# Weighted graph pass: one TensorE signal for each group of eight tiles, and GpSimd up to three groups ahead of the sums

## The reference, cut to what matters

```python
messages = edge_val[:, None] * embeddings[edge_src]
neighbor_emb = jax.ops.segment_sum(messages, edge_dst, num_segments=embeddings.shape[0])
```

## Time and profile before

| what | value |
|---|---|
| median of 3 runs | 9111.19 us (9107.15 to 9111.99) |
| profiled execution, its own time | 9109.78 us |
| its span, first to last instruction | 9108.0 us |
| mean granted TensorE clock | 0.752 of full |
| weighted pass, first gather to last addition | 4296.5 us to about 6910 us |
| gathers of the weighted pass | 1664, 950 ns each |
| scatters that stand between them | 164 |

### The profile page before, as it was taken

How to read it: one execution, slowest core, us unless ns; L and a number is a source line. 1 busy time by engine, 2 the same in 40 slices (tenths; PEclk the granted TensorE clock), 3 DMA queues, 4 the chain that set the end, 5 groups by cost and what they waited for, 6 DMA issues and landing times. The chain is left out here.

```text
span 9108.0 us, 108743 instructions
## 1 busy us (share of the span) xinstructions
PE 5754.6 (63%) x27644; PEld 4851.7 (53%) x27645; DVE 3952.2 (43%) x10086; ACT 1583.3 (17%) x3574; POOL 5514.8 (61%) x5737
## 2 busy tenths in 40 slices
PE   3677777777782588881444334444442489998994
PEld 3566656666662477771333333333332478888883
DVE  4566566777776400004444334444432432222225
ACT  1122121221120233330000000000000133333331
POOL 3566666666665466665666666666666246666662
PEclk7777777777775699995776776666766768888786
DMA  3333333333333144443332222222221022222335
GB/s 112 85 88 87 87 86 86 86 86 87 87 86 109 50 146 145 146 148 112 91 93 82 82 82 82 82 83 82 82 82 29 22 60 67 67 67 64 67 67 163
DMA packets 428356, 799.62 MB, mean 88 GB/s; under 512 B 129927, under 2 KB 267899, under 8 KB 427982
## 3 DMA queue, kind: packets, MB, share of 16 engines
q0 software_dynamic: 237808, 481.17, 21.3%
q1 hardware_dynamic: 190430, 317.21, 10.4%
HBM read 726.97 MB, written 70.98 MB: 88 GB/s over the span
## 5 line engine op out<-in xcount | busy, mean ns | idle before, releaser
L739 POOL DMA_INDIRECT g_G<-table,X x1664 | 1620.5, 974 | 944.0 <-issue 447.1
L1036 PE MATMUL g_pM<-g_G,g_S 128*128 128x256 f32 x3328 | 1111.0, 506 | 1674.8 <-DVE g_S L837 1371.4
L748 POOL DMA_INDIRECT g_G<-table,g_IDX x1664 | 1580.8, 950 | 843.2 <-issue 483.4
L1036 PEld LDWEIGHTS g_pM<-g_G,g_S 128*128 128x128 f32 x3328 | 854.2, 263 | 1931.6 <-DVE acc L857 1443.1
L1006 PE MATMUL g_pM<-g_G,g_S 128*128 128x260 f32 x3328 | 1205.7, 503 | 589.6 <-DVE acc L849 558.2
L1579 POOL DMA_INDIRECT q_G<-table,slot x1072 | 1038.1, 968 | 596.4 <-issue 288.3
L601 POOL DMA_INDIRECT slots<-sort_PAIR,sort_ADDR x1024 | 1011.8, 988 | 512.1 <-issue 310.7
L1006 PEld LDWEIGHTS g_pM<-g_G,g_S 128*128 128x128 f32 x3328 | 731.2, 241 | 904.9 <-DVE acc L849 674.6
L857 DVE TENSOR_TENSOR acc<-g_pM,acc 128x256 f32 x1664 | 698.3, 420 | 1172.8 <-remote 601.6
L849 DVE TENSOR_TENSOR acc<-g_pM,acc 128x260 f32 x1664 | 711.4, 428 | 477.9 <-remote 200.6
L837 DVE TENSOR_SCALAR g_S<-iota,g_REL,g_WT 128x128 f32<-128x128 f32 x1664 | 584.2, 352 | 388.7 <-issue 349.2
(11 more groups left out here) (320 smaller groups left out, 6979.0 us busy)
## 6 DMA issues: line engine op xcount, KB each, us to landing
e_W<-in_L_ffn_W SPq DMA_DIRECT2D x210, 512.0 KB
sort_PAIR<-slot_rows SPq DMA_DIRECT2D x66, 512.0 KB
g_G<-table,X POOLq DMA_INDIRECT x1664
g_G<-table,g_IDX POOLq DMA_INDIRECT x1664
ys_all<-ew_Y SPq DMA_DIRECT2D x196, 128.0 KB
sm_Y<-ys_all SPq DMA_DIRECT2D x28, 896.0 KB
q_ST<-slot_rows SPq DMA_DIRECT2D x34, 512.0 KB
sort_ADDR<-slot_rows SPq DMA_DIRECT2D x34, 512.0 KB
```

The source lines that it names most:

```text
L739: pool.indirect_dma_start(G[:, r, u, :], None, table, bass.IndirectOffsetOnAxis(ap=IDX[:, k * GRP + u:k * GRP + u + 1].bitcast(U32), axis= ...
L748: pool.indirect_dma_start(G[:, r, u, :], None, table, bass.IndirectOffsetOnAxis(ap=IDX[:, k * GRP + u:k * GRP + u + 1].bitcast(U32), axis= ...
L1036: m = pe.matmul(pM[r % 2 * 2 + half][:, u % HG, :], S[:, r, u, :], G[:, r, u, :], start=True, stop=True)
```

## The change

TensorE raises `sum` once a group instead of once a half. PSUM is laid out as two places of eight tiles (16 KB a partition together, as before), used in turn. VectorE waits once a group, for all eight products. GpSimd waits once a group, and `AHEAD` goes from 2 to 3: group `k` may be issued once group `k-3` has been multiplied. TensorE begins group `k` when all of group `k-2` has been added. The one-hots' own wait asks for the same group as before, in the new count.

```diff
-    AHEAD = 2
+    AHEAD = 3
...
-            pM = [sc.ps(f"{tag}_pM{j}", [P, HG, width]) for j in range(BANKS)]
+            pM = [sc.ps(f"{tag}_pM{j}", [P, GRP, width]) for j in range(2)]
...
                 for u in range(GRP):
-                    if u % HG == 0:
-                        at_least(pool, s["sum"], (k - AHEAD) * 2 + u // HG + 1)
+                    if u == 0:
+                        at_least(pool, s["sum"], k - AHEAD + 1)
...
-                    at_least(v, s["sum"], (k - RINGS + 1) * 2)
+                    at_least(v, s["sum"], k - RINGS + 1)
...
-            def add_of_half(rnd, r, u, blk):
+            def add_of_group(rnd, r, u, blk):
 
                 k = rnd * RINGS + r
-                if u % HG == 0:
-                    v.wait_ge(s["sum"], k * 2 + u // HG + 1)
+                if u == 0:
+                    v.wait_ge(s["sum"], k + 1)
                 at_least(v, s["added"], k * GRP + u)
-                v.tensor_tensor(node_sums(blk), pM[r % 2 * 2 + u // HG][:, u % HG, :], node_sums(blk),
-                                ALU.add).then_inc(s["added"], 1)
+                v.tensor_tensor(node_sums(blk), pM[r % 2][:, u, :], node_sums(blk), ALU.add).then_inc(s["added"], 1)
...
                 pe.wait_ge(s["onehot"], (k + 1) * GRP)
-                for half in range(2):
-                    at_least(pe, s["added"], (k - 2) * GRP + (half + 1) * HG)
-                    for u in range(half * HG, (half + 1) * HG):
-                        m = pe.matmul(pM[r % 2 * 2 + half][:, u % HG, :], S[:, r, u, :], G[:, r, u, :], start=True, stop=True)
-                    m.then_inc(s["sum"], 1)
+                at_least(pe, s["added"], (k - 1) * GRP)
+                for u in range(GRP):
+                    m = pe.matmul(pM[r % 2][:, u, :], S[:, r, u, :], G[:, r, u, :], start=True, stop=True)
+                m.then_inc(s["sum"], 1)
```

More of the change, by code:

```diff
@@ L920, in step_weighted @@
                         onehot(*after(rnd, r), u)
-                    add_of_half(rnd, r, u, blk[u])
+                    add_of_group(rnd, r, u, blk[u])
             if attend:
```

## The result

| what | before | after |
|---|---|---|
| median of 12 runs each, same chip | 9108.06 us (9098.93 to 9113.67) | 9125.44 us (9108.38 to 9134.03) |
| profiled execution, its own time | 9109.78 us | 9126.64 us |
| span | 9108.0 us | 9124.9 us |
| mean granted TensorE clock | 0.752 | 0.743 |
| weighted pass, first gather to end of last addition | 4296.45 to 6910.37, 2613.9 us | 4289.22 to 6915.15, 2625.9 us |

The ratio is 1.0018, 95% interval 1.001 to 1.0026: 17 us slower. I had forecast 9246, slower by 1.5%. The time lies inside the wide range that I gave (9000 to 9650), but just under the range for my likeliest case (9130 to 9480). The rival "the slack covers all" (9115) was right, with a small loss on top.

The account below looks back on a forecast made before the run. GpSimd's 18 DMA issues (22.3 us) plus a 3.3 us pause were taken to bound two groups. Slow additions on 164 groups at +0.8 us (+131) and start and end (+5) gave +136 on 9109.8: 9246 us, range 9000 to 9650.

Parts of the forecast that it names:

- my likeliest case: Drag exposed on VectorE: slow additions lengthen the path before TensorE's next group, around 9246 us; chance 0.47.
- the slack covers all: Rival: VectorE stays fast until t = 16, so the cycle's slack hides the longer path; 9115 us, chance 0.12.
- One signal a group, the walk: Serial TensorE and VectorE path from the late signal: 21.35 us for two groups instead of 16.60, beside a 25.6 us cycle.
- None costs 0. [...] I take the middle, three: Slow VectorE additions per two groups, bounds none and 5.5; three give 27.2 us, 13.6 a group, 0.8 over 12.8.
- the drag: After 11 to 17 us of unbroken indirect DMAs, TensorE's signals and VectorE's issue slow until GpSimd is quiet for 3.2 us.
- `AHEAD = 3` at nothing: GpSimd issuing one group further ahead still issues 18 DMAs in a row per two groups; costed at nothing.
- Start and end, +5: Start and end of the pass each expose one half's additions, about 2.4 us each: +5 us.
- All signals come at once: Rival: a single signal a group may escape being late, leaving GpSimd's 11.3 us a group; 8833 us, chance 0.17.
- The delay belongs to the signal: Rival: TensorE's second signal comes 9.3 us or more late whatever GpSimd does; 15.2 us a group, 9604 us, chance 0.08.
- Each signal waits for a pause: Rival: GpSimd stops after every nine issues, 14.5 us a group with scatters; 9469 us, chance 0.16.
- The clock: Rival: longer idle stretches leave all TensorE groups at half clock; alone +115 us over the forecast, nothing under the slack.
- The rule on rotating PSUM banks: Skill's rule: rotate independent matmul groups through PSUM banks so draining one overlaps the next's matmuls; its time is 9604 us.

## Why the prediction was wrong, step by step

- *What bounds the pass.* Right that GpSimd's stream with its pauses sets 12.8 us a group and TensorE's and VectorE's path has slack. Wrong that each unbroken run earns a quiet of 3.2 us. The pause is only what is left of 1.42 us for each DMA after issuing it in 1.25: 18 x 0.17 = 3.1.
- *One signal a group, the walk.* Right: 21.35 us forecast, 21.5 measured, and still inside a cycle of 25.6. Made the bound, it measured 20.5 for two groups.
- *The step that failed* is "None costs 0. [...] I take the middle, three": +0.8 on 164 groups, +131 us. The runs put 0 in its place: from group 45 to 207 the first gathers of the groups stand 12.80 us apart after and 12.82 before. Slow additions exist, in 28 of 164 groups, but only as the eighth, for which TensorE does not wait. I had tied the drag to the time since GpSimd's last resumption (11 to 17 us) on two cases, and had read these loosely. In the run from 5511.02 an addition at 5525.22 came after 2.71 us of "issue", 14.2 us after the resumption, and the next three were fast again, 0.59 us apart. Before a one-hot there were gaps of 0.77 us (5522.15) and 1.19 us (5539.86), longer than the 0.54 that I named. So the time since the resumption did not tell how many additions are slow. Most of the slow issue now falls behind the last addition, in VectorE's idle time. Why it falls there is not shown. With 21.5 us of path under 25.6, even two slow additions (3.9 us) would have been hidden, and nothing in the rows supported the middle of two bounds that far apart.
- *`AHEAD = 3` at nothing.* Right for the rate ("neutral if GpSimd still issues 18 in a row": it does), wrong by 10 to 11 us for the whole pass, by these profiles. GpSimd's stream from first to last gather takes 2601.0 us before and 2595.9 after (6897.47 and 6885.10 the last). But the last addition ends 12.9 us behind the last gather before, 30.1 us after, 22.5 with `AHEAD = 3` alone and 16.7 with the group signal alone. The stream that was allowed further ahead ended at most 5 us sooner, since its rate is the same, and those who follow it stand 10 to 17 us further behind, about one group.
- *Start and end, +5.* At the end all eight additions follow the last matmuls: 1 to 2 us in the pass with the group signal alone.
- *The 17 us.* The pass accounts for 12.0 in the two profiles; the pass began 7.2 us earlier in the profile after, and the stages behind it took some 12 us longer, in code that the change doesn't touch. I leave these to the spread (the kernel before ranged over 44 us in 28 runs on one chip). The whole-run ratios don't resolve `AHEAD = 3` alone: its interval ends at +7 us, short of the 11 that the one profile of its pass shows. The medians of the two parts are 2.7 and 4.2 us above the kernel before, 7 together and not 17; the two parts together were not run beside them. So the split of the 17 us rests on one profile of each kernel.
- *The rivals.* "All signals come at once": no, 313.3 us of GpSimd's stalls stay. "The delay belongs to the signal": no, 12.8 us a group, and the late signals now come 4.0 to 5.8 us after the group's last matmul where they came 9.1 to 11.9 us after it. "Each signal waits for a pause": no, GpSimd still issues 18 in a row in the steady part. Its argument against, that the first signals pass with little delay, was misread, though: 5545.48 is the second half of the group whose first is 5542.40, and in 71 of the 164 groups, all of them with a late second signal, the additions of the first half began 0.6 to 3.7 us after its matmuls. "The slack covers all": yes. The clock: TensorE's group of 3.72 us became 5.41, and the rise fitted under the slack, as that rival said.
- *The rule on rotating PSUM banks* (the Trainium skill, Perfetto Trace Analysis, Optimizing Tensor Performance) came to 9604 by itself. Its mechanism is real here, +3.0 us a group where GpSimd has five DMAs, and worth nothing where nine DMAs take longer than the pair of engines it speeds up.

## What to carry to other kernels

Before pricing a longer serial path, compare the whole of it with what the bounding engine needs for the same work: here 21.5 us beside 25.6, so the change cost nothing a group until the load of that engine fell, and then 600 us in all. Check also which instruction the next stage waits for: a late one behind it costs nothing. An unknown cost goes against the slack that is left (4.1 us), not straight into the sum. And when pauses fill in whatever time one adds or takes away, look for a rate: count the instructions over a long window before explaining a single pause.

## What the runs showed of the hardware that was not expected

- The same program took 9108 to 9227 us on some chips and 7693 to 7706 us on others. In the weighted pass this is 1.42 against 1.26 us for each indirect DMA, 12.8 against 11.3 us a group; other stages were faster as well: in the kernel after, 3597 against 4289 us ahead of the pass's first gather and 1797 against 2210 us behind its last addition.
- The rate of 1.42 us goes by the number of indirect DMAs, not by their bytes (1.42 at half width), and a memset or a wait between them doesn't relieve it. Each of these DMAs moves 128 rows, so the number of rows would fit as well; no run here varies it. Each signal that waits on it is passed when all DMAs issued so far have had theirs: six resumptions after 18, 24, 24, 32, 36 and 36 issues came at 1.41 to 1.42 us per issue.
- In the same traces VectorE issues slowly while the signals are late (the longest "issue" in front of a one-hot of 0.35 us is 4.1 us before and 4.4 after); on the faster chips the longest was 1.1 to 1.4 us.
- What causes the rate is open: it could belong to the chip or to how an execution is recorded there, and no run here tells these apart. One thing in the traces goes with it: the slower ones hold 3.1 to 3.7 semaphore updates for the landing of each gather, the faster ones 16.
